# Image patches of the fused kernel: nine full tiles in the front in place of one 72-row tile per pair

## What is computed

```
# x: 32 images -> 36 patches of 768 values each
t = layernorm(patches) * ln1_g + ln1_b          # over 768
t = t @ W_lin + b_lin                           # 768 -> 192
t = layernorm(t) * ln2_g + ln2_b                # over 192
h = concat([cls, t]) + pos_embedding[:37]       # 37 image rows
h = concat([h, txt])                            # + 128 text rows = 165 rows per image
h = h + linear_attention(layernorm(h))          # no softmax
u = layernorm(h); h = h + ffn_block(u)          # 12-head softmax attention, MLP, 4 experts top 2
```

## Time and profile before

| | |
|---|---|
| median of 3 runs | 1278.51 us (1276.96 to 1279.22) |
| span of the profiled execution | 1279.6 us |
| PE busy | 1201.2 us (94%) |
| VectorE busy | 939.3 us (73%) |
| ScalarE busy | 730.0 us (57%) |
| GpSimd busy | 412.7 us (32%) |
| mean granted TensorE clock | 0.989 |

### The profile page before, as it was taken

The page is one execution under the profiler, slowest core; times in us unless marked ns, Lnnn a source line. Parts: engine busy times, 40 slices in busy tenths (PEclk is TensorE's granted clock), DMA queues, the critical chain, the costliest instruction groups (busy, mean ns, idle before and its releaser), DMA issues.

```text
span 1279.6 us, 28412 instructions
## 1 busy us (share of the span) xinstructions
PE 1201.2 (94%) x9894; PEld 1025.9 (80%) x9894; DVE 939.3 (73%) x2602; ACT 730.0 (57%) x1705; POOL 412.7 (32%) x397
## 2 busy tenths in 40 slices
PE   7899999999999999999998899999999999999994
PEld 6777777777777777777776799998888899899993
DVE  4677787777777787778767678777778877776773
ACT  1256555555566545655557655554656666667661
POOL 2101110111111110111010027877568644455444
PEclk8899999999999999999999999999999999999997
DMA  3481122202120122112400524346477677667652
GB/s 106 122 214 37 38 64 56 64 16 57 56 64 21 51 64 57 39 34 64 96 18 9 206 47 81 79 90 159 118 190 196 169 179 183 164 159 171 183 143 30
DMA packets 95387, 124.51 MB, mean 97 GB/s; under 512 B 9382, under 2 KB 87591, under 8 KB 91343
## 3 DMA queue, kind: packets, MB, share of 16 engines
q1 hardware_dynamic: 71743, 102.48, 26.7%
q0 software_dynamic: 23568, 21.06, 10.9%
HBM read 70.68 MB, written 52.83 MB: 97 GB/s over the span
## 4 chain that ended last, share of the span: by engine, by line
PE 61%; DVE 13%; issue 10%; POOL 5%; DMA 5%; ACT 5%; DVEq 0%; POOLq 0%; SPq 0%; ACTq 0%
PE PS L1634 49%; PE PS L1637 12%; DMA out<-YO,ids 4%; POOL out L769 2%; DVE K L1182 2%; POOL expert_rows L732 1%; DVE st L1094 1%; DVE rec L1204 1%; ACT PT L787 1%; DMA consts<-in_attn_const 1%; ACT XAT L787 1%; ACT GF L980 1%; DVE CN L1205 1%; ACT PX L812 1%; DVE ZS L1152 1%
## 5 line engine op out<-in xcount | busy, mean ns | idle before, releaser
L1634 PE MATMUL PS<-w2r,GH 128*120 (+1 forms) x828 | 247.6, 362 | 2.4 <-DVE GL L1359 1.2
L659 POOL TENSOR_TENSOR rs<-ve,minus_half 128x3 f32<-128x3 f32 (+1 forms) x80 | 58.8, 736 | 558.6 <-DVE ve L1099 558.6
L769 POOL DMA_INDIRECT out<-YO,ids x94 | 160.9, 1712 | 147.0 <-DVE flag L1575 64.0
L1634 PE MATMUL PS<-w2r,GL 128*120 (+1 forms) x828 | 208.0, 251 | 0.0
L812 ACT ACTIVATE PX<-PS,nb 128x165 f32<-128x165 f32 x576 | 177.1, 417 | 47.6 <-DVE nb L1170 45.9
L980 ACT ACTIVATE GF<-PS,b1c 128x480 f32<-128x480 f32 (+1 forms) x216 | 137.8, 638 | 81.9 <-PE PS L1634 79.5
L1634 PE MATMUL PS<-XH,w1r 128*128 128x480 f32 (+1 forms) x432 | 168.9, 393 | 7.2 <-ACT GF L980 4.4
L1634 PEld LDWEIGHTS PS<-w2r,GH 128*120 128x120 f32 x828 | 150.2, 181 | 5.9 <-DVE GL L1359 4.0
L1634 PEld LDWEIGHTS PS<-w2r,GL 128*120 128x120 f32 x828 | 152.4, 184 | 0.0
L1175 DVE COPY PT<-PS 128x384 f32<-128x384 f32 x144 | 80.3, 557 | 87.0 <-PE PS L1637 83.5
L1637 PE MATMUL PS<-ident,PX 128*128 128x128 f32 x864 | 130.5, 281 | 7.3 <-ACT PT L787 5.4
(11 more groups left out here) (270 smaller groups left out, 2332.6 us busy)
## 6 DMA issues: line engine op xcount, KB each, us to landing
w1r<-expert_w_parts SPq DMA_DIRECT2D x25, 1536.0 KB, 7.4
expert_rows<-empty SPq DMA_DIRECT2D x45, 369.4 KB, 5.7
RT<-expert_rows SPq DMA_DIRECT2D x22, 369.4 KB, 3.9
X<-x_scratch SPq DMA_DIRECT2D x11, 360.0 KB, 3.9
out<-X POOLq DMA_DIRECT2D x11, 360.0 KB, 5.6
XP<-in_patches SPq DMA_DIRECT2D x32, 108.0 KB
H<-in_txt SPq DMA_DIRECT2D x16, 192.0 KB, 3.9
out<-H SPq DMA_DIRECT2D x16, 192.0 KB
```

Source lines behind the costliest of these rows:

```text
L659: nc.gpsimd.tensor_tensor(rs[:, k - 1, 0:n], ve[:, k - 1, 0:n], eps_half[:, 0:n], ALU.pow).then_inc(rstd_ready[k - 1], 1)
L769: nc.gpsimd.indirect_dma_start(out[:, :], bass.IndirectOffsetOnAxis(ap=ids[:, i, t:t + 1], axis=0), YO[:, i % 2, t, :], None, bounds_check ...
L1634: return nc.tensor.matmul(o, l, r, start=start, stop=stop)
```

## The change

All 1152 patch rows are worked in the front as nine tiles of 128 rows (PTILES), in four load buffers (PBUF), their steps put by hand between those of pair 0. Work is dealt anew among the engines:

- The mean is subtracted on ScalarE (`centred`), in place; the division by the standard deviation is moved behind the product, into `token_stats` on VectorE (factor prs). The patch weights with their gain go to a tile of their own (wpatch), made by VectorE (four of six) and ScalarE (two).
- The second norm is applied by ScalarE (`ynormed`), GpSimd multiplies with the gain and adds to the position rows (`patch_tokens`), to which it has added the bias (`positions`). Tile 0 alone is finished by VectorE (`first_patch_tokens`).
- Copies of bias rows, high halves of the pair weights go to ScalarE; the zeroing of K and Q to GpSimd; the two constant tensors are loaded in two parts each.
- Finished tokens are stored to device memory (`store_tokens`), one DMA per tile, each after a wait for its token. With each pair's text two DMAs load its 36 + 36 token rows (`load_tokens`); pair 0 takes them from tile 0 directly.
- The pair bodies lose the patch step on all engines; most fillers of the front go too.

```diff
+        def load_tokens(i):
+            for b in range(2):
+                sp.dma_start(H[64 * b + 1:64 * b + NIMG, 2, :], tokd[bass.ds((2 * i + b) * NPATCH, NPATCH), :]).then_inc(txt_in, 16)
+        def store_tokens(t):
+            sp.wait_ge(token_ready, t + 1)
+            if t == 0:
+                first_tokens()
+            sp.dma_start(tokd[P * t:P * t + P, :], TK[:, 1 + t, :]).then_inc(token_stored[min(t // 2, 1)], 16)
...
         for k in range(2):
             sp.dma_start(ow[64 * k:P, k, :], a["out_wT"][P * k:P * k + KD[k], :]).then_inc(ow_in, 16)
-        load_text(0)
+        for t in range(PTILES - PBUF):
+            load_patches(t + PBUF)
+            store_tokens(t)
...
             if more:
                 load_text(i + 1)
+                load_tokens(i + 1)
...
-        next_patches(1)
-        next_patches(2)
+        sp.wait_ge(token_stored[0], 32)
         h1_store(0, True)
+        for t in range(PTILES - PBUF, PTILES):
+            store_tokens(t)
...
+        def patch_tokens(t):
+            pool.wait_ge(ynorm_ready, t)
+            y = YN[:, t % 3, :]
+            nc.gpsimd.tensor_tensor(y, y, g2, ALU.mult).then_inc(yscaled_ready, 1)
+            pool.wait_ge(yscaled_ready, t)
+            pool.wait_ge(token_ready, t)
+            nc.gpsimd.tensor_tensor(TK[:, 1 + t, :], TK[:, 1 + t, :], y, ALU.add).then_inc(token_ready, 1)
...
+        def token_stats(t):
+            dve.wait_ge(prstd_ready, t + 1)
+            dve.wait_ge(tok_ps, t + 1)
...
+            steps.link(stt(y, PS[:, token_bank(t), 0:D], prs[:, t:t + 1], lin_bias[:, :], ALU.mult, ALU.add))
...
         def tokens(j):
 
-            dve.wait_ge(rstd_ready[1], j + 1)
-            steps.link(stt(Y2[:, :], Y[:, :], mv[:, 1, 0, 0:1], g2m[:, :], ALU.subtract, ALU.mult))
-            steps.link(stt(H[:, 2, :], Y2[:, :], rs[:, 1, 0:1], b2m[:, :], ALU.mult, ALU.add))
-            dve.wait_ge(txt_in, j * 16 + 16)
+            dve.wait_ge(txt_in, j * 48 + 48)
             stats(j, 3, lambda t: H[:, t, :], 3)
```

More of the change, by code:

```diff
@@ L667, in residual, with body @@
             last.then_inc(ub_ready, 1)
-        def body(i, lin=True, patch=True, core=True, first=False):
-            if lin:
+        def body(i, lin=True, first=False):
+            if lin and not first:
                 rstd(i + 1, 3, 3)
[L673 to L676, removed]
+            residual(i, first)
             if lin:
@@ L933, in body @@
                 w1_high(3)
+        bias_rows()
+        centred(0)
+        patch_weights(range(4, KP))
         xnT(0)
+        centred(1)
+        xnT(1)
+        centred(2)
         scores_of_tokens()
-        body(-1, core=False)
+        xnT(2)
+        ynormed(1)
+        weights_high()
+        xaT(0)
+        centred(3)
+        lin_y(0, 0)
+        lin_y(0, 1)
+        xnT(3)
+        ynormed(2)
+        centred(4)
+        lin_v(0)
+        xnT(4)
+        ynormed(3)
+        centred(5)
+        lin_m(0)
+        value_bias_T()
+        centred(6)
+        ynormed(4)
+        xnT(5)
+        centred(7)
+        xnT(6)
+        ynormed(5)
+        xnT(7)
+        centred(8)
+        ynormed(6)
+        zT(0)
+        xnT(8)
+        queries(0)
+        ynormed(7)
+        ynormed(8)
         body(0)
@@ L1228, in w2_low, with body @@
             tt(w2r[:, f, :, D:2 * D], rw2[:, f, :, :], w2r[:, f, :, 0:D].bitcast(F32), ALU.subtract).then_inc(w2lo_ready, 1)
[L1230 to L1235 removed]
+        def body(i, lin=True, more=True, first=False):
+            maxima(i, 0)
+            if not first:
+                x1_out(i - 1)
             if lin:
                 lin_in(i + 1)
[L1238 to L1240 removed]
+            values(i)
+            if lin:
                 probsT(i, 0)
@@ L1302, in body @@
                 w1_low(3)
-            if patch:
+            if more:
                 tokens(i + 2)
         patch_stats(0)
-        patch_normed(0)
-        rows_of_biases()
-        patch_weights()
+        patch_weights(range(0, 4))
+        patch_stats(1)
+        patch_bias()
         token_stats(0)
+        class_rows()
+        first_patch_tokens()
+        patch_stats(2)
+        token_stats(1)
         tokens(0)
-        body(-1, core=False)
+        lin_in(0)
+        own_masks()
+        patch_stats(3)
+        token_stats(2)
+        pair_biases()
+        weights_low()
+        patch_stats(4)
+        token_stats(3)
+        patch_stats(5)
+        patch_stats(6)
+        token_stats(4)
+        patch_stats(7)
+        lin_out(0)
+        output_bias()
+        token_stats(5)
+        u_stats(0, True)
+        token_stats(6)
+        z_out(0)
+        patch_stats(8)
+        token_stats(7)
+        z_low(0)
+        dve.wait_ge(qk_zeroed, 1)
+        keys(0, 2)
+        keys(0, 1)
+        tokens(1)
+        token_stats(8)
         body(0, first=True)
         before = steps.base + steps.k
-        N_STEPS = 16
+        N_STEPS = 9
         with dve.Fori(1, PAIRS - 2) as i:
```

664 lines of the change are left out of this document (395 added, 269 removed).

## The result

The changed kernel takes 1285.27 us (median of 17 runs, 1283.98 to 1291.15) against 1279.22 us (17 runs, 1275.84 to 1284.47) on the same chips: a ratio of 1.0056, 95% interval 1.0043 to 1.0069, so 5.5 to 8.8 us slower. The profiled execution has a span of 1286.4 us, against 1279.6.

A forecast was written before the change was run, and what follows sets the result against it. TensorE, at 41.5 us a pair, was taken to bound the kernel. Pair 1's delayed maxima +20.8, half clock +2.0, pairs -15.7 and -2.8 gave +4.3 us: 1282.8 us, range 1267 to 1290.

The forecast's parts named there:

- The pairs: Pair bodies without the patch step: 1.21 us less in each of 14 pairs, 0.23 us at 12 starts, together -19.7 us.
- The front: Nine patch tiles instead of two before the first exponentials: these at 68.5 us for 60.65, +7.8 us (+4 to +13).
- the walk: Stepping through the front's four engine queues in the changed order, instruction by instruction: first exponentials at 68.5 us.
- SyncE's list: Vectors, weights, fills and pair 2's text, issued behind tile 8's store: starts at 70.4, lands at 119.9 us.
- The half clock: TensorE at half speed for 4 us after standing some 12 us in pair 1: 2.0 us more.
- The sum: Whole kernel: +20.8 + 2.0 - 15.7 - 2.8 = +4.3 us, 1282.8 us for the median.
- Rival A: Faster: pair 2's rows land by 104.6, wait small or absent: 1266.6 us, with half the wait 1274; chance 0.19.
- Rival B: Slower still: heavier front, GpSimd slowing VectorE's norms, first exponentials after 73 us: 1288 us; chance 0.14.
- Rival C: The pairs give the patch step's whole 3.2 us on TensorE, period 38.3 us: 1257 us; chance 0.04.
- The forecast's wait for the rows: VectorE waits 15.3 us for pair 2's rows before statistics of H at about 105, released by a DMA.
- the 1.2 us for PT: TensorE's wait of about 1.2 us for the copy PT before each pair's second context product, from pair 2 on.
- the text's issue: SyncE issues the load of pair 2's text near 112 us.

The follow-up runs named there:

- e10: The kernel before, with PT copy number 14 moved from VectorE to ScalarE in every pair: 1289.77 us against 1289.59, ratio 0.9999.
- e5: e1 with tile 8's token statistics behind the first maxima and values, and its norm behind the first two exponentials: ratio 0.9934.
- e8: e1 with GpSimd's bias additions to the position rows left out for token tiles 1 to 8 (8 of 25 additions): ratio 0.9945.
- e3: The kernel before, with the patch step left out of pairs 0 to 13 on all engines: 1260.96 us, ratio 0.9882.
- e4: The kernel before, with one added wait: SyncE's list starts only after the first pair's first exponentials: 1292.09 us, ratio 1.0107.
- e6: e1 with TensorE transposing the identity in five waits of the front and the first pair: ratio 0.992.
- e1: The changed kernel, with SyncE's stores of token tiles 5 to 8 issued behind its list and pair 2's text and tokens: 1270.54 us, ratio 0.9942.
- e2: The changed kernel, with SyncE's seven fills moved behind pair 2's text and tokens: 1274.68 us, ratio 0.9961.
- e7: e1 with PT copy number 14 moved from VectorE to ScalarE in every pair: 1273.65 us where before takes 1289.84, ratio 0.9879.
- e12: The same program as e1, repeated beside the later runs: ratio 0.9933.

## Why the prediction was right

The forecast was 1282.8 us and slower at 0.61; the median is 1285.3. Step by step:

- **The pairs: right.** Forecast 1.21 and 0.23 us a pair, for pairs 1 to 13 15.7 + 2.8 = 18.5; measured 13 x (41.53 - 40.18) = 17.6. Taking pair 14 of the old kernel as the comparison, and not the step's busy time, was the right reading, and e10 says why: VectorE's chain bounds one kind of pair and not the other.
- **The front: right against the profile, its terms not.** Forecast 68.5 us, measured 68.72, and the chain at its end is the one that was named (GpSimd's step and tile 8's norm, e5). But the walk gave VectorE 46 us of work and 11 of waiting; from 5.9 us to its first maxima at 66.26 it was busy 40.5 us and stood 19.9. Three waits for TensorE's token products alone took 5.3 us, the longest 3.4, where the walk's longest for such a product was 2.2. The two misses have opposite signs, so the hit to 0.2 us is in part luck.
- **SyncE's list: right.** Forecast first vector 70.4, measured 70.54; forecast rows at 119.9, measured 121.29. The list was 50.75 us long and not 49.5: with the same landing, 1.2 of the 3 us missed. VectorE's wait was 16.2 for 15.3, the maxima at +22.1 for +20.8.
- **The half clock: undersized.** Forecast 2.0 us, by assuming that 4 us at half speed follow; the rows show 4 us at 0.50 and four more at 0.65, and by the score products they cost 2.75 us. Another 0.75 us.
- **The sum.** +22.1 + 2.75 - 17.6 = +7.3 us, where the forecast had +4.3. The three misses, +1.3, +0.75 and +0.9, lay on the same side.
- **Rival A fell** on its deciding point: the list landed 16.7 us past 104.6. For the stretch of the list the kernel after shows 245 GB/s at a share of 1.01. The Trainium skill, DMA: Bandwidth & Descriptors, Specifications, has some 358 GB/s as the limit of memory for a core. At 245 the trace stays below it for this list, and the shorter list that rival A's estimate takes from that figure did not come.
- **Rival B fell** with 68.72 for 73 and with e8. **Rival C fell** with the period of 40.18 for 38.3 (e3).
- The forecast's wait for the rows and its release by a DMA, the 1.2 us for PT, the text's issue (113.95 for 112) were all seen.

One more thing was right by luck. The profiled execution of before had a slow front (last section), and so the cost of the new front read smaller than against an old front at full clock; the profiled execution of after was 3.0 us above its median (1288.26 for 1285.27) and the one of before 2.9 above the 1278.51 it was set against (its time is its span and 1.8 us), so the two offsets cancelled.

## What to carry to other kernels

Moving work out of a loop also moves every queue that it is issued on: look for what stands behind it in order. Here that was a load far back in the same list, and not the moved work itself. A store that waits for late data should be issued behind everything that waits for nothing, down to the first reader. And before pricing a step that leaves a loop, find which engine bounds the loop without it; a spare engine may take one copy and turn 1.35 us into 2.0.

## What the runs showed of the hardware that I had not expected

**A short wait costs TensorE as much clock as a long one.** After 15.14 us, 13.91 us and 2.62 us of standing, the next score product took 2.02 us each time (1.11 at full clock), and the loss up to the next pair was 2.75 us, 1.8 in the kernel with the patch step (e4), and 2.77. So taking 12.5 us off a wait left its last 2.8 in place.

**The old front is not one length.** Four traces have its code on the engines. In e4 SyncE's list starts only behind it, and e3 leaves out one load of patches. In the order before, e3, e4, e10, their windows, and for e4 and e10 the first exponentials:

```profile
0.00:57.00 57.00, 45.61 (x257) 38.93 (x258) 27.03 (x98) 10.38 (x24) 9.82 (x31) 0.88 0.30 90
```

```profile
0.00:57.00 57.00, 45.80 (x275) 38.21 (x276) 29.31 (x109) 11.61 (x26) 9.80 (x31) 0.94 0.30 91
```

```profile
0.00:57.00 57.00, 44.05 (x289) 37.19 (x290) 30.78 (x110) 11.84 (x27) 11.07 (x33) 1.00 0.19 68
56.77 1.84 ACT L813 ACTIVATE PX<-PS,nb 128x165 f32<-128x165 f32 x6 [1.82 <-DVE nb L1171]
```

```profile
0.00:57.00 57.00, 44.21 (x298) 37.20 (x300) 31.44 (x111) 12.58 (x30) 11.81 (x35) 1.00 0.35 107
56.04 1.85 ACT L812 ACTIVATE PX<-PS,nb 128x165 f32<-128x165 f32 x6 [1.81 <-DVE nb L1170]
```

At a granted clock of 0.88, 0.94, 1.00 and 1.00 the first exponentials come at 60.65, 58.20, 56.77 and 56.04 us. The new front, in the six traces without the edits of e5 or e6 (after, e1, e2, e7, e8, e12), gives 68.10 to 69.32. Set against the old front at full clock the new one costs 12 us and not 8. e10 has everything that before has, so the missing list of e4 is not the reason. It fits that e1 shows 10.1 us of gain up to the first MLP product against the profile of before, and only 7.4 by the timed runs. What decides which clock an execution of the old front gets is open.

**An issue right behind large transfers takes longer.** The H1 store's first issue took 0.40 us in e1, 5 us after the last fill had been issued, 2.00 us in the changed kernel, right behind the fills, and 4.01 us in e2, right behind the weight loads. The first of the fills, behind the weight loads, took 2.7 to 4.1 us (e1, e4, after, before) and 0.37 in e2, where it follows the text. It fits a queue that is full; no row shows its length.
